# Keys and values of the second layer: their bias enters PSUM by a two-row product, and ScalarE instead of VectorE moves them out

## The reference

```python
qkv = (x @ w_qkv + b_qkv).reshape(B, HW, HEADS, 3 * HEADC)
qkv = qkv.transpose(0, 2, 1, 3)
q, k, v = jnp.split(qkv, 3, axis=-1)
k = _ln(k, kln_g, kln_b)
v = _ln(v, vln_g, vln_b)
kv = jnp.einsum('bhnd,bhne->bhde', k, v) / HW
out = jnp.einsum('bhnd,bhde->bhne', q, kv)
```

## Time and profile before

| | |
|---|---|
| three runs | 2613.03, 2618.08, 2610.80 us, median 2613.03 |
| profiled execution | 2613.48 us, span on the core 2611.7 us |
| PE busy | 2328.2 us, 89% |
| DVE busy | 1840.5 us, 70% |
| ACT busy | 1412.8 us, 54% |
| POOL busy | 1290.1 us, 49% |
| the stage of the change | 1828 to 1926 us |

### The profile page before, as it was taken

How to read it: one execution, slowest core, us unless ns; L and a number is a source line. 1 busy time by engine, 2 the same in 40 slices (tenths; PEclk the granted TensorE clock), 3 DMA queues, 4 the chain that set the end, 5 groups by cost and what they waited for, 6 DMA issues and landing times. The chain is left out here.

```text
span 2611.7 us, 47485 instructions
## 1 busy us (share of the span) xinstructions
PE 2328.2 (89%) x16074; PEld 2180.5 (83%) x16074; DVE 1840.5 (70%) x4683; ACT 1412.8 (54%) x3105; POOL 1290.1 (49%) x1446
## 2 busy tenths in 40 slices
PE   7788999889998999899699779985888899899988
PEld 6668999889988998899577679974788899799977
DVE  6666787677767777665677656548887677777765
ACT  4334666456645665455564344445334677567766
POOL 1203554255525543465687446641767567566600
PEclk9989999999999999999899579998999899899999
DMA  5111111211121112122532344546666377467711
GB/s 118 49 34 39 47 43 44 65 46 44 46 68 41 46 45 65 32 59 59 122 92 79 107 140 158 157 110 185 186 186 176 111 214 216 126 186 213 208 55 57
DMA packets 157064, 266.08 MB, mean 102 GB/s; under 512 B 40070, under 2 KB 101423, under 8 KB 156696
## 3 DMA queue, kind: packets, MB, share of 16 engines
q0 software_dynamic: 51504, 150.65, 20.9%
q1 hardware_dynamic: 105320, 112.38, 14.5%
HBM read 226.12 MB, written 36.83 MB: 101 GB/s over the span
## 5 line engine op out<-in xcount | busy, mean ns | idle before, releaser
L1045 POOL DMA_INDIRECT gat<-table,srcT x400 | 414.4, 1036 | 340.0 <-DVE m L2985 189.3
L1213 POOL DMA_INDIRECT x_rows<-table,srcT x392 | 406.1, 1036 | 213.6 <-issue 81.1
L681 PE MATMUL pa<-w,act 128*125 128x256 f32 x2400 | 359.7, 288 | 15.5 <-DVE act L2742 15.2
L681 PE MATMUL pb<-hT,w 128*128 128x378 f32 (+1 forms) x1920 | 335.9, 311 | 1.0 <-DVE hT L2818 1.0
L681 PEld LDWEIGHTS pa<-w,act 128*125 128x125 f32 x2400 | 314.9, 188 | 20.4 <-DVE act L2742 20.3
L681 PEld LDWEIGHTS pb<-hT,w 128*128 128x128 f32 x1920 | 286.4, 189 | 3.2 <-DVE hT L2818 1.8
L2742 DVE TENSOR_TENSOR act<-gf,act 128x378 fp32r<-128x378 f32 (+1 forms) x320 | 153.7, 483 | 106.0 <-ACT act L2121 104.2
L2118 ACT ACTIVATE gf<-pb,b1s 128x378 f32<-128x378 f32 (+1 forms) x320 | 165.6, 518 | 109.7 <-PE pb L681 97.2
L681 PE MATMUL pa<-fw,actb 128*125 128x256 f32 x1200 | 168.9, 282 | 4.2 <-DVE actb L3769 3.9
L2427 ACT ACTIVATE gf<-pb,bne 128x378 f32<-128x378 f32 (+1 forms) x215 | 130.3, 606 | 73.2 <-PE pb L681 61.7
L681 PEld LDWEIGHTS pa<-fw,actb 128*125 128x125 f32 x1200 | 152.7, 186 | 7.8 <-DVE actb L3769 7.8
(11 more groups left out here) (553 smaller groups left out, 5990.3 us busy)
## 6 DMA issues: line engine op xcount, KB each, us to landing
e<-in_L_ffn_W_dram SPq DMA_DIRECT2D x40, 512.0 KB, 4.9
spill<-m SPq DMA_DIRECT2D x80, 170.0 KB
msg<-spill SPq DMA_DIRECT2D x40, 340.0 KB
fraw<-in_L_ffn_W_dram SPq DMA_DIRECT2D x48, 256.0 KB
w1r<-in_L_mix_W_dram SPq DMA_DIRECT2D x7, 1024.0 KB, 5.1
gat<-table,srcT POOLq DMA_INDIRECT x400
x_rows<-table,srcT POOLq DMA_INDIRECT x392, 3.7
fraw<-in_L_ffn_Wo_dram SPq DMA_DIRECT2D x24, 256.0 KB
```

Source lines behind the costliest of these rows:

```text
L681: mm = nc.tensor.matmul(ps, lhs(l), rhs(r), start=first and n == 0, stop=last and n == 2)
L1045: pool.indirect_dma_start(out=gat[:, i % 2, c, :], out_offset=None, in_=table0, in_offset=bass.IndirectOffsetOnAxis(ap=srcT[:, i * GC + c: ...
L1213: pool.indirect_dma_start(out=x_rows[:, n % UB, c, :].bitcast(F32), out_offset=None, in_=table1, in_offset=bass.IndirectOffsetOnAxis(ap=sr ...
```

## The change

The bias enters the product. Two rows of `act_[1]` hold the negated bias, its upper part in row 0 and its lower part in row 1, for keys and for values, and 125 columns of minus one in the same two rows. A product of those two rows opens the accumulation of each key or value tile (`kv_product`), in front of the six products, which no longer start it. The two rows are made by DVE in unit 15 of the experts' stage (`keep_bias`). DVE's `kv_add` goes; ACT copies each finished bank from PSUM to `kv` (`kv_evict`), at the head of its step, ahead of the squares.

```diff
--- before.py
+++ after.py
@@ -590,6 +590,8 @@
         C_BIAS.append(C_SOFT[-1] + 1 + 3 * len(part))
     bias_items = [[(k, i) for k in range(len(part)) for i in range(3)] for part in PARTS]
 
+    kv_bias = act_[1][0:2, :, :].rearrange("p a c -> p (a c)")[:, 0:2 * D]
+    kv_minus = act_[1][0:2, 3, 0:TP]
     cw_parts = hn[:, :, :].rearrange("p t d -> p (t d)")
     unit_banks = [[pa[:, i] for i in range(3)], [pt[:, i] for i in range(2)]]
     kv_banks = [pg[:, 0], pb[:, 1]]
@@ -1845,9 +1847,11 @@
         def kv_product(t, k):
 
             pe.wait_ge(s["y_used"], Y_L1 + 2 * t + k + 1)
+            to = pa[0:TP, (2 * t + k) % 3, 0:D]
+            nc.tensor.matmul(to, kv_minus, kv_bias[:, k * D:(k + 1) * D], start=True, stop=False)
             for h in range(H):
-                last = hi_lo_products(pa[0:TP, (2 * t + k) % 3, 0:D], lambda l: xT[l][:, t // GT, h, t % GT * TS:t % GT * TS + TP],
-                                      lambda r: kvw[r][:, h, k, :], h == 0, h == H - 1)
+                last = hi_lo_products(to, lambda l: xT[l][:, t // GT, h, t % GT * TS:t % GT * TS + TP],
+                                      lambda r: kvw[r][:, h, k, :], False, h == H - 1)
             last.then_inc(s["y_ps"], 1)
 
         def kv_sums(t):
@@ -2407,9 +2411,19 @@
             table_upper(t + 4)
         for j in range(GT):
             act.wait_ge(s[f"t1_st{j}"], 32 * NG)
+        def kv_evict(t, k):
+
+            n, b = 2 * t + k, 4 * (t % GT) + 2 * k
+            if t >= GT and k == 0:
+                act.wait_ge(s["g7"], t - GT + 2)
+            act.wait_ge(s["y_ps"], Y_L1 + n + 1)
+            nc.scalar.activation(kv[:, b:b + 2, 0:P], pa[0:TP, n % 3, 0:D].rearrange("p (h c) -> p h c", h=H), ACT.Copy).then_inc(s["y_used"], 1)
+
         for n in range(NT + 1):
             if n < NT:
                 j = n % GT
+                for k in range(2):
+                    kv_evict(n, k)
                 act.wait_ge(s["y_used"], Y_L1 + 2 * n + 5)
                 nc.scalar.activation(kvq[:, j, :, :].rearrange("p k (h c) -> p (k h) c", h=H), kv[:, 4 * j:4 * j + 4, 0:P], ACT.Square
                                      ).then_inc(s["sq_go"], 1)
@@ -3495,6 +3509,16 @@
             for k in range(2):
                 split([w[:, h, k, :].rearrange("p (a c) -> p a c", c=AD) for w in kvw], w3[:, :, (k + 1) * AD:(k + 2) * AD])
 
+        def keep_bias():
+
+            rows = bkv[0:2, :].rearrange("p (a x) -> p a x", x=3 * AD)
+            me(nc.vector.tensor_scalar(kv_minus, ones[0:2, 0:TP], -1.0, None, ALU.mult))
+            for k in range(2):
+                of = rows[:, :, (k + 1) * AD:(k + 2) * AD]
+                to = kv_bias[:, k * D:(k + 1) * D].rearrange("p (a c) -> p a c", c=AD)
+                me.link(dve, nc.vector.tensor_copy(to, of))
+                me.link(dve, nc.vector.scalar_tensor_tensor(to, to.bitcast(F32), ident[0:2, 1:2], of, ALU.mult, ALU.subtract))
+
         x_keep(0)
         for f in range(MT):
             up_lower(1, f)
@@ -3519,6 +3543,8 @@
                 split_weights(u - 11)
             if u in (13, 14):
                 split([w[:, u - 13, :] for w in awx], aw[:, u - 13, :])
+            if u == 15:
+                keep_bias()
         keep_y(NUN - 1)
         dve.nop().then_inc(s["f_lo"], NUN * MT)
         dve.nop().then_inc(s["y_used"], 2 * NUN)
@@ -3665,17 +3691,6 @@
                     mr.join(dve)
         dve.nop().then_inc(s["rb_sum"], 1)
 
-        def kv_add(t, k):
-
-            if t >= GT and k == 0:
-                dve.wait_ge(s["g7"], t - GT + 2)
-            n, b = 2 * t + k, 4 * (t % GT) + 2 * k
-            dve.wait_ge(s["y_ps"], Y_L1 + n + 1)
-            nc.vector.tensor_tensor(kv[:, b:b + 2, 0:P].rearrange("p h (a c) -> p h a c", c=AD),
-                                    pa[0:TP, n % 3, 0:D].rearrange("p (h a c) -> p h a c", h=H, c=AD),
-                                    bkv[:, :].rearrange("p (h a x) -> p h a x", h=H, x=3 * AD)[:, :, :, (k + 1) * AD:(k + 2) * AD],
-                                    ALU.add).then_inc(s["y_used"], 1)
-
         def kv_squares(t):
 
             j = t % GT
@@ -3696,9 +3711,6 @@
         me.join(dve)
         nc.vector.tensor_copy(qT[:, :, :], pt[:, :, 0:D]).then_inc(s["dve7"], 1)
         for n in range(1, NT + 3):
-            for k in range(2):
-                if n <= NT:
-                    kv_add(n - 1, k)
             if n <= NT + 1 and kv_group(n - 1) is not None:
                 add_windows1(kv_group(n - 1))
             if 2 <= n <= NT + 1:
```

## The result

The changed kernel takes 2618.13 us in the median of 20 runs, the kernel before 2612.47 us beside it, also in 20: ratio **1.0025, 95% interval 1.0015 to 1.0035**. By the ratio it is some 6.5 us slower (5.7 by the two medians), where 2611.0 was forecast and 2617.0 was the end of the range. The profiled execution has a span of 2610.4 us, shorter than that of before (2611.7).

The account below looks back on a forecast made before the run. POOL's self-paced row gathers were taken to bound the second mixer's stage, DVE only its tail. Tail -0.75 and long gathers -1.3 us made -2.0, from a median of 2613.0 to 2611.0 us; range 2606.5 to 2617.

Parts of the forecast that it names:

- Bias products: 50 two-row products added on PE, 0.118 us each, 5.9 us in all, covered by PE's waits for gathers.
- Rival 2: In the key and value loop PE becomes late and POOL's ring waits: slower, 2618.0 us, chance 0.13.
- Long gathers: POOL's 60 gathers lose the random value, 3.8 us, where 5.1 were measured: -1.3 us, bounds -5.1 and +3.8.
- Tail: After the last gathered chunk, the last tile's pair of bias additions leaves DVE's serial path: -0.75 us.
- ACT's evictions: 50 PSUM-to-SBUF evictions added on ACT, 383 ns each, 19.2 us in all, hidden: 0 taken, bounds 0 and 19.2.
- keep_bias at nothing: Five short DVE operations in unit 15 of the experts' stage, at most 2.1 us, covered: 0 taken.
- POOL paces the kernel before, not DVE: 60 self-paced gathers, 80.0 us, set the second mixer's loop until 1914.39; DVE's additions ahead of that are worth nothing.
- Rivals 1 and 3: In the loop, long gathers vanish: 2607.2 us, chance 0.15; or DVE was the bound after all: 2594.3 us, chance 0.04.

Follow-up runs that it names:

- e3: Changed kernel with its two-row bias product, but DVE instead of ACT copies the key and value banks out; 2621.42 us, ratio 1.0031.
- e14: Changed kernel with its two-row bias product, DVE doing each reduction to mean squares twice; 2622.46 us, ratio 1.003.
- e13: Changed kernel with a bias product of 128 rows, zeros cleared in two pieces, and DVE doing each reduction twice; 2616.32 us, ratio 1.0008.
- e1: Changed kernel with a bias product of 128 rows, 126 of them zeros cleared by one DVE operation in unit 15; 2621.83 us, ratio 1.004.
- e9: Changed kernel with a bias product of 128 rows, zeros cleared in two smaller pieces in unit 15, keep_bias in unit 17; 2615.21 us, ratio 1.0017.
- e10: Changed kernel with a bias product of 128 rows, zeros cleared in two pieces, and each DVE scaling in two halves; 2612.93 us, ratio 1.0002.
- e2: Changed kernel without the bias product, the bias left out of keys and values, ACT still evicting; 2615.24 us, ratio 1.0007.
- e4: Changed kernel with a tile's two two-row bias products issued one after the other, ahead of its twelve others; 2615.19 us, ratio 1.0004.
- e12: Changed kernel run again unaltered, for a second trace; 2619.60 us, ratio 1.0028.
- e11: Kernel before the change with only each DVE scaling split in two halves; 2609.94 us, ratio 0.9995.

## Why the prediction was wrong

The changed kernel is slower by **the cost of the bias product on PE, which is enough for nearly the whole loss by itself**. PE takes 11.8 us for three tiles at 3.30 and two window groups at 0.94 (eight products each), gapless, and those groups use eight gathers; eight gathers with their gaps take 10.0 us when none is long. Short gathers therefore only turn into waits for PE and a late last group (e3, e14), and with the same gathers e13 is 7.2 us shorter in the stage than e14. **Long gathers stand beside it**: with PE relieved and gathers left long the stage stays at 97.3 and 98.7 us (e1, e9), with PE relieved and at most 5.8 us lost in gathers it is 92.5 to 94.5 (e10, e13, e2; e4 has half the steps and few long gathers). Why PE's relief came with long gathers in e1 and e9 and not in e2 is open.

Point by point, by the steps of the prediction:

- *Bias products, "the bounds are 0 and 5.9", covered.* **This is the step that failed first.** The price came from products with 125 rows among their like; there was no row of a product with few rows between products with all, and "two rows may cost less than 125 to load" took fewer rows as cheaper at worst. A step with no row needed a wider bound. It costs 0.50 us where 0.118 was taken, some 25 us over the stage or 6 in each 25, twice the 3 of 25 that PE stood idle before.
- *Rival 2, late PE, slower.* PE did become late, and its chance of 0.13 was too low. But its sign, gathers that wait for PE in the ring, isn't there in the changed kernel (0 us beyond the gaps, 0.5 in e12): the gathers were long enough to hide it, and it shows only in e3 and e14. That its 2618.0 us falls beside the measured 2618.1 is luck: its price was a quarter of the true one, and instead of showing at one chunk, PE was late everywhere.
- *Long gathers, "-1.3", bounds -5.1 and +3.8.* The second step that failed: +4.4 us. What makes a gather long was right, and its size too (remaining time less 0.13). Wrong was to take the starts as random. They follow DVE's rhythm, and the removed additions were part of that rhythm, by 2.1 us as counted above; what brought the other 2.3 is open.
- *Tail, "-0.75".* Seen in e2, 0.63 us. In the changed kernel it went under: the last chunk was issued at 1912.89 us, and with the shortest and the median time to landing, 3.3 and 3.7 us, it was there by 1916.2 to 1916.6 (an estimate); PE came to its group at 1917.64, and the tail grew by 0.8 us.
- *ACT's evictions, 383 ns, hidden.* Right: 378 ns, where the plain copy on DVE takes 417 (e3), and e2 shows no price. *keep_bias at nothing.* Right for its five short operations; e1 shows that one of 1.32 us in unit 15 isn't free.
- *POOL paces the kernel before, not DVE.* Right, by e11: DVE has as much to do and a little more, and shorter gathers alone take 2.4 us off the stage. Rivals 1 and 3 are out: the long gathers grew, and DVE's 19 us less brought nothing.

What stays open: by the ratios, all variants on the first kind of chip but e1 stand 0 to 2.3 us above what their stage says, against the one trace of before, e11 among them. That may be this trace of before or something behind the stage. Also open is what decides how many gathers are caught: 9 in e4 and 16 in e2, against 21 to 24 in e1, e9, e12 and the changed kernel, all without the additions. No run varied the phase of DVE against POOL alone.

## What to carry to other kernels

Look at who is next before freeing an engine: DVE's additions were idle weight for the path, but they spaced out scalings, which lengthen the gathers that start inside them. A matmul that uses few of the array's rows isn't small among full ones: it cost four times a full one, so pad it with rows of zeros (100 did) or put such products together. And price an operation that has no row of its own kind from above by a measurement first, not by a bigger operation of another shape.

## What the runs showed of the hardware

- Between matmuls over 128 rows at the full granted clock, one over 2 or 64 rows takes 0.31 us and delays the six behind it by 0.19 to 0.21; one over 100 or 128 rows takes 0.12 and delays nothing. With 2 rows the weight loads don't run ahead across the step, in either direction.
- An indirect gather on GpSimd that starts inside a VectorE operation with two SBUF inputs ends 1.49 to 1.53 us after that operation's start (operation 0.67 to 0.69, gather alone 0.95), for offsets of 0.045 to 0.51 us. Six gathers that started 0.012 to 0.035 us into a scaling (e13, e14) took 0.95 to 0.96, and the scaling 0.04 to 0.07 us longer instead; but one 0.024 us into a one-hot took 1.47 (e11). Two such operations 1.66 to 1.69 us apart therefore can catch one gather after the other at 0.14 us.
- With 17 us more VectorE work between such operations a stage was 4.6 us shorter (e13 against e9, one execution each).
- On the second chip the kernel before took 2666.94 us instead of 2612 and engines stood still for up to some 5 us without a named releaser; ratios of 0.3% couldn't be read from it.
